# Scaling the sorted key values and adding up the candidate cells on GpSimd instead of VectorE, in a fused convolution, attention and product-key expert kernel

## The reference

```python
    s0 = einsum('bshq,eq->bshe', _l2norm(q0), _l2norm(keys0))   # 8 heads, 64 keys
    s1 = einsum('bshq,eq->bshe', _l2norm(q1), _l2norm(keys1))
    sc0, ix0 = top_k(s0, K)                                     # K = 16
    sc1, ix1 = top_k(s1, K)
    cs = (sc0[..., :, None] + sc1[..., None, :]).reshape(b, s, H, K * K)
    ci = (ix0[..., :, None] + ix1[..., None, :]).reshape(b, s, H, K * K)
    fs, pos = top_k(cs, K)
    fi = take_along_axis(ci, pos, axis=-1)
    w = softmax(fs, axis=-1)
    inner = einsum('bsd,bshkd->bshk', hidden_states, expert_down[fi])
    act = gelu(inner, approximate=False)
    out = einsum('bshk,bshko->bso', act * w, expert_up[fi])
```

## Time and profile before

| | before |
|---|---|
| median of 3 executions | 451.5 us (449.02 to 451.69) |
| profiled execution | 449.87 us |
| its span | 447.8 us, 7841 instructions |
| DVE busy | 358.4 us (80%) |
| PE busy | 308.1 us (69%) |
| POOL busy | 217.9 us (49%) |
| ACT busy | 140.7 us (31%) |
| mean granted TensorE clock | 0.701 of full speed |

### The profile page before, as it was taken

One profiled execution on the slowest core, in us unless ns is written; L12 is line 12 of the kernel. 1 busy time (PEld: TensorE's weight loads), 2 busy tenths in 40 slices (PEclk: granted clock), 3 DMA queues, 4 the chain that ended last, 5 costly groups with the idle time before them and its releaser, 6 DMA issues.

```text
span 447.8 us, 7841 instructions
## 1 busy us (share of the span) xinstructions
PE 308.1 (69%) x2275; PEld 225.2 (50%) x2275; DVE 358.4 (80%) x2163; ACT 140.7 (31%) x324; POOL 217.9 (49%) x411
## 2 busy tenths in 40 slices
...
DMA packets 1634, 3.50 MB, mean 8 GB/s; under 512 B 180, under 2 KB 1205, under 8 KB 1592
## 3 DMA queue, kind: packets, MB, share of 16 engines
...
...
## 4 chain that ended last, share of the span: by engine, by line
DVE 55%; PE 23%; POOL 9%; issue 6%; ACT 6%; DMA 1%; DVEq 0%; ACTq 0%; POOLq 0%
PE bank L876 6%; DVE Sx L1363 5%; DVE i L1369 5%; DVE i L1370 5%; DVE cands L1419 4%; DVE onehot L494 4%; DVE vraw L1366 3%; DVE vraw L1360 3%; DVE segmax L1244 3%; DVE c L1416 3%; PE bank L540 2%; PE bank L550 2%; DVE masked L1426 2%; PE bank L783 2%; ACT hat L914 2%
## 5 line engine op out<-in xcount | busy, mean ns | idle before, releaser
L876 PEld LDWEIGHTS bank<-weights,onehot 108*128 108x128 f16 x1024 | 69.0, 178 | 3.1 <-DVE onehot L494 1.5
L876 PE MATMUL bank<-weights,onehot 108*128 108x16 f16 x1024 | 69.0, 216 | 1.9 <-DVE onehot L494 1.4
L1644 POOL TENSOR_TENSOR inv<-nrm,mhalf 128x16 f32<-128x16 f32 x8 | 23.4, 2925 | 35.8 <-DVE nrm L1376 35.8
L458 POOL TENSOR_TENSOR taps<-qpad,wa 128x128 f32<-128x128 f32 x96 | 36.0, 427 | 2.0 <-ACT qpad L929 1.9
L540 PE MATMUL bank<-wa,hat 128*128 128x128 f32 x24 | 6.7, 371 | 32.9 <-ACT hat L914 32.9
L1557 POOL TENSOR_TENSOR rstd<-veps,mhalf 128x2 f32<-128x2 f32 x16 | 11.7, 731 | 34.6 <-DVE veps L1166 34.3
L1370 DVE FIND_INDEX8 i<-vraw,Sx 128x8 uint16<-128x64 f32 x128 | 28.0, 219 | 0.0
L1369 DVE FIND_INDEX8 i<-vraw,S 128x8 uint16<-128x64 f32 x128 | 28.0, 218 | 0.0
L1363 DVE MATCH_REPLACE8 Sx<-vraw,S 128x64 f32<-128x64 f32 x128 | 25.1, 209 | 0.0
L803 PE MATMUL bank<-KB,qsT 128*128 128x256 f32 x64 | 24.9, 558 | 0.2 <-issue 0.2
L494 DVE TENSOR_SCALAR onehot<-eT 108x512 f16<-108x512 uint16 x84 | 24.4, 366 | 0.0
...
## 6 DMA issues: line engine op xcount, KB each, us to landing
...
bq_row<-rows_dram SPq DMA_DIRECT2D x1, 0.5 KB
...
```

The source lines that it names most:

```text
L458: ins = eng.tensor_tensor(tv[:, :, :, ky, kx:kx + n], q, dw[:, ky, kx:kx + n].unsqueeze(1).unsqueeze(1).broadcast_to([P, G8, G8, n]), ALU. ...
L876: last = mm(o[:, g * 16:g * 16 + 16], OHv[:, c * NT + t, g], Rv[:, c, t, g, s], start=(c == 0 and s == 0), stop=(c == NCH - 1 and s == 1))
L1644: g_.tensor_tensor(inv[:, n], nrm[:, n], mhalf[:, 0:2 * H], ALU.pow).then_inc(inv_ready, 1)
```

## The change

The function `sums` leaves the DVE program, where only a wait on a new semaphore `cand_ready` is left of it, and goes to the POOL program as the new stages N2g (tile 0) and N2h (tile 1). The arithmetic is the same. On POOL the scaling waits for the sorted values (`i16_ready`) and for `inv`, then the five additions follow behind a wait of the engine on itself. `cells` on POOL needs no wait for `v16` any more, since it stands behind `sums` on the same engine. The list "vector" is unchanged. In "gpsimd" N2g and N2h are put in; "tensor" and "scalar" are new, with 14 W in place of 21, and so is `BANKS`.

```diff
-BANKS = """01234560124536012453601245360242513460460251304625130462513620423643501643250254
...
+BANKS = """01234560132456013245601325601325602415315315602431560243156430236421056421305142
...
-        v16_ready = sem("v16_ready")
+        cand_ready = sem("cand_ready")
...
 @block.vector
             def sums(b, t):
-
-                n, h = slice(t * 2 * H, t * 2 * H + 2 * H), slice(t * H, t * H + H)
-
-                dve.wait_ge(inv_ready, NT * b + t + 1)
-                dve.wait_ge(i16_ready, NT * b + t + 1)
-                v.tensor_tensor(v16[:, h, :, :].rearrange("p g a k -> p (g a) k"),
-                                vraw[:, h, :, :].rearrange("p g a k -> p (g a) k"),
-                                inv[:, n].unsqueeze(2).broadcast_to([P, 2 * H, TOP]),
-                                ALU.mult).then_inc(v16_ready, 1)
-                dve.wait_ge(v16_ready, NT * b + t + 1)
-                for i0, r, c, at in CELL_BLOCKS:
-                    last = v.tensor_tensor(cand[:, h, at:at + r * c].rearrange("p g (r c) -> p g r c", r=r),
...
-                link(last)
+                dve.wait_ge(cand_ready, NT * b + t + 1)
...
 @block.gpsimd
+            def sums(b, t):
+
+                n, h = slice(t * 2 * H, t * 2 * H + 2 * H), slice(t * H, t * H + H)
+                if b >= 1:
+                    pool.wait_ge(onehot_dve_ready, b)
+                    pool.wait_ge(wem_ready, NT * b)
+                pool.wait_ge(i16_ready, NT * b + t + 1)
+                pool.wait_ge(inv_ready, NT * b + t + 1)
+                link(g_.tensor_tensor(v16[:, h, :, :].rearrange("p g a k -> p (g a) k"),
+                                      vraw[:, h, :, :].rearrange("p g a k -> p (g a) k"),
+                                      inv[:, n].unsqueeze(2).broadcast_to([P, 2 * H, TOP]), ALU.mult))
+                for i0, r, c, at in CELL_BLOCKS:
+                    last = g_.tensor_tensor(cand[:, h, at:at + r * c].rearrange("p g (r c) -> p g r c", r=r),
+                                            v16[:, h, 0, i0:i0 + r].unsqueeze(3).broadcast_to([P, H, r, c]),
+                                            v16[:, h, 1, 0:c].unsqueeze(2).broadcast_to([P, H, r, c]), ALU.add)
+                last.then_inc(cand_ready, 1)
+
+            def N2g(b):
+                sums(b, 0)
+
+            def N2h(b):
+                sums(b, 1)
...
             def cells(b, t):
 
                 h = slice(t * H, t * H + H)
-                pool.wait_ge(v16_ready, NT * b + t + 1)
```

More of the change, by code:

```diff
@@ L109 @@
 ORDERS = {
[L110 to L121, removed]
```

46 lines of the change are left out of this document (27 added, 19 removed).

## The result

| | before | changed |
|---|---|---|
| median, 12 executions each | 450.91 us (449.02 to 452.71) | 453.37 us (451.88 to 454.98) |
| profiled execution | 449.87 us, span 447.8 | 452.32 us, span 450.5 |

The ratio is 1.0054, 95% interval 1.0033 to 1.0074: 2.5 us slower, inside the 1% that I had called no change. The forecast was 453.5 us.

What follows compares the result with a forecast made beforehand. DVE was taken to bound the kernel (55% of the span). Losses and gains over the places summed to +3.0 us, added to a mean of 450.5: 453.5 us; range 450 to 457 alone, 447 to 459 with rivals and bounds.

Steps and rivals of the forecast that it cites:

- fourth rival: GpSimd takes 2.6 us at a place; six uncovered hand-offs cost 0.3 more each: 455.3 us; chance 0.07.
- The sum of the waits: DVE's six waits for POOL's sums come to 13.6 us, against 12.8 us of work taken off DVE.
- place 7: Image 3, both tiles: POOL's sums stand behind tile 1's power and tile 0's cells, DVE waits; loss 4.5 us.
- Places 1 and 2: Image 0, tiles 0 and 1: DVE sheds 1.75 us at each, part lost to TensorE's chain; gain 1.4 us together.
- Place 3: Image 1, tile 0: a DVE wait of 0.4 us takes the place of 1.3; gain 0.9 us.
- Place 4: Image 1, tile 1: uncovered hand-off loses 0.6 us, ACT's new order 0.8 more; loss 1.4 us.
- Places 5 and 6: Image 2: tile 0 partly covered by one product, loss 0.4 us; tile 1 uncovered, loss 0.6 us.
- Place 8: End of TensorE: the filler between the two scatters goes, another outlasts ACT's copy by 0.4; gain 0.5 us.
- Place 9: The start: fewer fillers delay TensorE, gain 0.7 us; 0.4 more for image 3's first normalization, done earlier by ACT.
- Gains are kept: Image 0 tile 1 yields 3.5 us, ACT's order in image 1 costs nothing, start 0.9 more: 449.7 us; chance 0.18.
- New lists pay: The new TensorE and ScalarE orders, not the move, take 8 us from TensorE's chain: 445.5 us; chance 0.08.
- Lower clock: TensorE drops to its lower clock before F10a.0 and F11b.3, matmuls behind take twice as long: 458.5 us; chance 0.22.

Runs made afterwards that it cites:

- e2_move_alone: The changed kernel with the TensorE and ScalarE lists and bank table of the kernel before: 455.28 us, ratio 1.0105 to the kernel before.
- e4_mixed: The changed kernel with the sums of image 1 tile 1, image 2 and image 3 back on DVE: 449.36 us, ratio 0.9964 to the kernel before.
- e9b_power_between: The changed kernel with GpSimd's last-image list reordered, tile 1's power and both sums ahead of tile 0's cells: 449.34 us, ratio 0.9979 to the kernel before.
- e3_lists_alone: The kernel before with the new TensorE and ScalarE lists and bank table, sums still on DVE: 450.84 us, ratio 0.9994 to the kernel before.
- e10b_tail_covered: The changed kernel with the last image reordered on TensorE, DVE and GpSimd: 443.52 us, ratio 0.9840 to the kernel before.

## Why the prediction came out right, step by step

- **Price of the moved work.** Scaling took 0.61 to 0.63 us and the five additions 1.55 us (1.63 and 1.64 at two places); the cells are there 2.25 us after POOL starts and 2.5 after the sorting. These are the 2.3 and 2.4 of the rows, not the 2.6 of the fourth rival. The factor of about 2 in the Trainium skill (GPSIMD Engine Reference, section 4.1, Engine selection) would have given that 2.6 as well. The measured ratio is 1.7, 2.25 us on POOL to 1.34 on DVE where POOL is quiet (scaling 0.42, additions 0.89, with a gap), and the measurement decides.
- **The sum of the waits.** The 13.6 us of the prediction has a slip: at place 7 it counts the first wait from 394.96, where DVE marked before. With its sums gone DVE stands still from 393.60, so this wait is 4.2 us and not 2.8, and the six come to 15.0. That is what was measured, 15.0, with 4.04 at this place. The forecast of the time does not use the term.
- **Places 1 and 2** were sized too small: 1.4 us together; the lead grew by 1.8 at each, and by 2.2 up to image 1's sorting. I let F11a.1's wait take most of it. It did wait (0.9 us), but only for itself: the work of other stages behind it started early all the same, so the lead at 184 us was 3.9. Another 1.15 us went in the next attention (between 220 and 238 us), which I had not counted. 2.2 less 1.15 is 1.05: the sum was near the 1.4, the path to it was not.
- **Place 3**: 0.9 forecast, 0.9 measured, with a wait of 0.21.
- **Place 4**: the hand-off cost 0.6, as said, and 0.9 more went behind it, for the 0.8 that I had put on ScalarE's order. The size was luck, the cause was wrong. The copy L952 did move, as forecast, behind the exponential, to 245.90 us, but DVE's marking outlasts what hangs on it, and e2_move_alone, with the old order, loses the same 0.9 us. The trace shows where: DVE's rows of the slots at 261.4 wait for ACT (1.62 us, before 1.11), ACT for TensorE, and TensorE for POOL's merge, which ends at 257.06 in place of 258.58, a lead of 1.5 where DVE had 2.4. So POOL's own list, longer by the sums, ends last there. In e4_mixed, with these sums on DVE, nothing is lost between the same rows.
- **Places 5 and 6**: 0.65 and 0.6 for 0.4 and 0.6.
- **Place 7**: 4.4 us for 4.5, by the order named. e9b_power_between takes it away.
- **Place 8**: 0.9 for 0.5; the filler between the scatters was worth all it took, 0.86, and the one at the end cost nothing that shows. e3_lists_alone, with the new TensorE list and no move, wins 0.8 there, and e2_move_alone, with the old list, wins nothing.
- **Place 9**: the start's 0.7 is not shown: the 1.1 us in the profile is within what the start varies, with either set of lists. Image 3's first normalization came out 0.6 for 0.4, but by luck, as the rest of two larger things that I had not seen. They stand in these rows, before and then changed:

```profile
354.33 8.99 DVE L494 TENSOR_SCALAR onehot<-eT 108x512 f16<-108x512 uint16 x28
355.50 7.28 POOL L494 TENSOR_SCALAR onehot<-eT 108x512 f16<-108x512 uint16 x4
```
```profile
354.18 5.74 DVE L493 TENSOR_SCALAR onehot<-eT 108x512 f16<-108x512 uint16 x28
353.75 6.22 POOL L1618 TENSOR_TENSOR qrstd<-ssq,mhalf 128x8 f32<-128x8 f32 x1 [0.39 <-DVE ssq L1327]
355.36 10.58 POOL L493 TENSOR_SCALAR onehot<-eT 108x512 f16<-108x512 uint16 x4
```

DVE's 28 masks ran through in 5.74 us in place of 8.99, and the second query normalization behind them is 3.2 us earlier. But POOL stood meanwhile: its power took 6.22 us (1.77 before), its four masks end 3.2 us later, the scatter N5a.2 that needs them starts at 366.0 in place of 364.5, and DVE waits 2.3 us for TensorE's scores, which stand behind that scatter. This is not the change's doing alone: e3_lists_alone, with the sums on DVE, has 5.74 and the wait, e2_move_alone and e4_mixed have 9.0 and no wait. What decides between the two is open. In e10b_tail_covered the masks take 5.74 too, but the scores stand ahead of the scatter, and the wait is gone.

- **Rivals.** "Gains are kept": place 2 did yield, but the next attention took 1.15 us back. "New lists pay" falls with e3_lists_alone: nothing by the median, and hardly 1 us if the lower level in its trace is left out. "Lower clock": the level dropped in both of its places. At F10a.0 and F10b.0 the 32 matmuls took 2.09 + 1.74 us in place of 1.59 + 1.15. The granted clock was 0.50 up to 82 us, where the kernel before had 0.72 from 80 to 82 and 1.00 from there. DVE's wait behind them went from 7.37 to 9.39; it is a part of the start, whose lead fell from 2.7 to 0.7 there. At F11b.3 L766 took 1.22 in place of 0.71. The two together are 1.6 us of matmuls, under the 2.5 that the rival needed. The clock matters in a third, the queries of image 2, where the changed kernel met the higher level.

So the largest term, place 7, is right in mechanism and size, and so are the price and place 3, and nearly so places 5 and 6. Place 4's second half, places 1 and 2 and image 3's normalization are right in size by luck.
